# Summing edge attributes two chunks at a time in a graph network kernel: 64 or 128 stationary columns per product

## The chip, the cores and the metric

The kernel runs on one core of a Trainium2 chip. The metric is the device time of one execution in microseconds (us), as the median of a few runs. Five engines work side by side: TensorE (PE in the profile, with its weight loads in a row of their own, PEld), VectorE (DVE), ScalarE (ACT), GpSimd (POOL) and SyncE (SP), which here only issues transfers.

## The reference, cut to what matters

A graph with 6,250 nodes and 206,250 edges (self loops among them, sorted by destination) goes through two residual blocks. The first is two graph convolutions, the second an MLP whose input for each node is its own 128 features, the sum of the 64 attributes of all edges that end in it, and a constant vector.

```python
agg = jax.ops.segment_sum(edge_attr, col, num_segments=x.shape[0])   # (206250, 64) -> (6250, 64)
h = jnp.concatenate([x, agg, u[batch]], axis=1)
h = leaky_relu(h @ w1 + b1)
h = leaky_relu(h @ w2 + b2)
return h @ w3 + b3
```

The change is about `agg`, and about the one product of the MLP that reads it. All of this is in float32.

## The kernel before, in words

The program has stages that are separated by barriers.

**The first stage** does two things at once. One is the sum `agg`. The other is preparation: ScalarE counts where each node's edges begin (`count_rows`, `recount_rows`), GpSimd gathers rows of the edge list for it with indirect transfers (`rows`), VectorE and ScalarE normalise the nodes (`stats`, `mean_var`, `shift`, `h`), TensorE turns them (`turn_nodes`), and ScalarE and GpSimd split them into two halves in float16 (`scaled`, `g_hi`, `g_lo`).

For the sum the edges are cut into 162 runs of 1280 edges. A run lies on 128 partitions with 10 edges each, and "chunk" c of a run is the c-th edge of every partition, 128 edges with 64 attributes. The edges are sorted, so a run touches few nodes: VectorE compares each edge's destination, taken relative to the run's first, with 0..43 and gets a 0/1 matrix `hot` of 128 x 44 for each chunk (`make_hot`). TensorE multiplies the chunk's attributes (`arows`, the stationary operand, 64 columns) with the chunk's `hot` (the moving operand, 64 columns, of which 44 count) and adds the ten chunks of a run up in PSUM (`agg_p`). VectorE then adds the 44 columns into the resident sum `agg` at the run's first node (`add_unit`), which it reads from `base_i` into a register. The adds of two runs can touch the same nodes, so each waits for the one before it (`s_moved`).

Three runs are a unit, six units are a turn, and nine turns cover all edges: 54 units. The units are written out in the same order on each engine. SP loads the attributes of a unit (0.96 MB) into one of 6 buffers, VectorE makes `hot` two units ahead into one of 3 buffers, TensorE sums a unit in `sum_unit` into one of 3 banks. Before a unit TensorE waits for the load, for `hot` and for VectorE's adds of the unit three before. Part of the units stand in loops, and from the third turn on (the fourth for TensorE) they are written out singly, numbered m on VectorE and TensorE, with preparation work put between them: `stats` after m = 0 to 6, `mean_var` at 7, `shift` at 14, the edge codes at 15 and 16, transposes of nodes on TensorE from m = 15 on. The last turn runs in a loop of its own after all of this.

**The last stage**, the second layer with the MLP, goes over the nodes in 13 steps (one of 128 nodes, then 12 of 512). In each step TensorE does 98 products for the second convolution (`multiply`), and the short products of the MLP for the step before are put between them (`stages`). The one that reads `agg` is in `turn_to_nodes`. The weights come in `load_weights`, from SP's queue, and every engine waits for all of them (`s_w`).

Between these two lie the building of the adjacency matrix and the first convolution, which the change does not touch.

Of the kernel before, what the change touches and what calls it, by code (L numbers as in the profile page):

```python
# [17 lines left out]
ALU = mybir.AluOpType  # L18
ACT = mybir.ActivationFunctionType
AX = mybir.AxisListType  # L20
F32 = mybir.dt.float32
# [4 lines left out]
P = 128  # L26
N, F = 6250, 128
E = 206250
HI = -(-N // P)
NP = HI * P  # L30
# [21 lines left out]
AC = 10  # L52
AE = P * AC
AT = -(-E // AE)
OVER = AT * AE - E
AH = AT // 2
AW = 44
AQ = 3
AU = 6
AS = 3  # L60
AK = 512 // AH
TURNS = AT // (AQ * AU)
TA, TB_, TC_, TC = 2, 3, 7, 7
# [2 lines left out]
GB = 5  # L66
SPLIT = [(k, min(GB, HI - k)) for k in range(0, HI, GB)]
EF = 64
HOT = AQ * AC * AW + EF - AW

EC = E // P
ET = E - P * EC
# [10 lines left out]
EPS = 1e-5  # L83
ROUNDS = -(-E // P) + 1
AROUNDS = -(-NP // AW)
assert OVER % AC == 0 and 0 < OVER < AE and TURNS * AQ * AU == AT and TC == TURNS - 2 and AU % AS == 0


def build(nc, x, src, dst, attr, W1, b1, W2, b2, u, w1, c1, w2, c2, w3, c3, out):
    with ExitStack() as top:  # L90
        def sb(name, shape, dt, ctx=top):
            return ctx.enter_context(nc.sbuf_tensor(name, shape, dt))

        def ps(name, shape, ctx):
            return ctx.enter_context(nc.psum_tensor(name, shape, F32))
# [25 lines left out]
        scale2 = sb("scale2", [P, 1], F32)  # L121
        inv2 = sb("inv2", [P, 1], F32)
        W1_sb = sb("W1_sb", [P, F], F32)
        agg = sb("agg", [EF, NP + AW], F32)
        b1_sb = sb("b1_sb", [P, 1], F32)

        class Chain:
# [92 lines left out]
        with ExitStack() as ph:  # L220
# [35 lines left out]
            arows = sb("arows", [P, AU, AQ, AC, EF], F32, ph)  # L256
            hot = sb("ahot", [P, AS, HOT], F32, ph)
            arel = hot[0:AH, :, :].rearrange("q s n -> q (s n)")[:, 0:2 * AE].rearrange("q (t e) -> q t e", t=2)
# [7 lines left out]
            agg_p = ps("agg_p", [P, AS, 512], ph)  # L266
# [44 lines left out]
            s_w = sem("s_w1", ph)  # L311
# [10 lines left out]
            s_moved = sem("s_moved", ph)  # L322
# [125 lines left out]
            def _(dve):  # L448
# [12 lines left out]
                def add_unit(r, i, k):  # L461

                    n = (r * TURNS + i) * AU + k
                    at = [dve.value_load(base_i[0:1, bass.ds((i * AU + k) * AQ + q, 1)], min_val=0, max_val=NP)
                          for q in range(AQ)]
                    dve.wait_ge(s_summed, n + (AU + 1))
                    for q in range(AQ):
                        dve.wait_ge(s_moved, n * AQ + (q + AS * AQ))
                        nc.vector.tensor_tensor(agg[:, bass.ds(at[q], AW)], agg[:, bass.ds(at[q], AW)],  # L469
                                                agg_p[0:EF, k % AS, q * EF:q * EF + AW], ALU.add).then_inc(s_moved, 1)  # L470

                def unit(i, k):

# [123 lines left out]
                with dve.Fori(0, rounds) as r:  # L597
                    start = first_turn(dve, r)
# [133 lines left out]
            def _(pe):  # L732
                pe.sem_inc(s_summed, AU)

                def sum_unit(r, i, k):
                    n = (r * TURNS + i) * AU + k
                    gate(pe, s_loaded[k], (r * TURNS + i + 1) * (32 if k == 0 else 16))
                    gate(pe, s_hot, n + 1)
                    gate(pe, s_moved, n * AQ + AQ)
                    for q in range(AQ):  # L740
                        for c in range(AC):
                            e = (q * AC + c) * AW
                            ins = nc.tensor.matmul(agg_p[0:EF, k % AS, q * EF:(q + 1) * EF], arows[:, k, q, c, :],  # L743
                                                   hot[:, k % AS, e:e + EF], start=(c == 0), stop=(c == AC - 1))
                    ins.then_inc(s_summed, 1)

                def sum_turns(a, b):
# [19 lines left out]
                for f, (t, c, n) in enumerate(AFILL):  # L767
# [3 lines left out]
                    for k in range(n):  # L771
                        ins = nc.tensor.transpose(tp[:, f % 2, k * AH:(k + 1) * AH],
                                                  arel[:, t, :].rearrange("q (p c) -> q c p", c=AC)[:, c + k, :],
                                                  ident[0:AH, 0:AH])
# [36 lines left out]
                with pe.Fori(0, rounds) as r:  # L811
                    start = first_turn(pe, r)
# [394 lines left out]
        def second_layer_and_mlp():  # L1207
# [3 lines left out]
            M1, M2 = w1.shape[1] // P, w2.shape[1] // P  # L1211
            assert M1 == M2
            KU = F + EF
# [5 lines left out]
            with ExitStack() as ph:  # L1219
# [20 lines left out]
                W_sb = sb("W2_sb", [P, F], F32, ph)  # L1240
                b_sb = sb("b2_sb", [P, 1], F32, ph)
                w1a = sb("w1a", [P, M1 * P], F32, ph)
                w1b = sb("w1b", [EF, M1 * P], F32, ph)
                w1u = sb("w1u", [EF, M1 * P], F32, ph)
                w2_sb = sb("w2_sb", [P, M1, M2 * P], F32, ph)
                w3_sb = sb("w3_sb", [P, M2, F], F32, ph)
# [11 lines left out]
                s_w = sem("s_w2", ph)  # L1258
# [48 lines left out]
                @block.sync  # L1307
                def _(sp):
                    def load_weights(sp):
                        sp.dma_start(W_sb[:, :], W2).then_inc(s_w, 16)  # L1310
                        sp.dma_start(w1a[:, :], w1[0:F, :]).then_inc(s_w, 16)
                        sp.dma_start(w1b[:, :], w1[F:KU, :]).then_inc(s_w, 16)
                        sp.dma_start(w1u[:, :], w1[KU:KU + EF, :]).then_inc(s_w, 16)
                        sp.dma_start(w2_sb[:, :, :], w2.rearrange("(m p) n -> p m n", p=P)).then_inc(s_w, 16)
                        sp.dma_start(w3_sb[:, :, :], w3.rearrange("(m p) n -> p m n", p=P)).then_inc(s_w, 16)
                        with nc.allow_non_contiguous_dma(reason="vectors, one element per partition"):
                            sp.dma_start(b_sb[:, :], b2.rearrange("(p a) -> p a", a=1)).then_inc(s_w, 16)  # L1317
                            sp.dma_start(c3_sb[:, :], c3.rearrange("(p a) -> p a", a=1)).then_inc(s_w, 16)
                            sp.dma_start(u_sb[:, :], u[0:1, :].rearrange("a n -> n a")).then_inc(s_w, 16)
                            sp.dma_start(c1_sb[:, :], c1.rearrange("(m p) -> p m", p=P)).then_inc(s_w, 16)  # L1320
                            sp.dma_start(c2_sb[:, :], c2.rearrange("(m p) -> p m", p=P)).then_inc(s_w, 16)

                    def program(sp, one_round):
                        def load(i, h, n):
                            c = i * 2 + h
                            w = n * P
                            cols = bass.ds(first_node(i, h), w)
                            if one_round and two_before(i):

                                gate(sp, dense_done, c + 1)  # L1330
                                sp.dma_start(adj_in[:, h, :, 0:w], adj_d[:, :, cols]).then_inc(adj_ready[h], 16)

                            if two_before(i):
                                gate(sp, y_added, c + 1)
                                gate(sp, stored[h], i * 16)
                            sp.dma_start(cur[:, h, 0:w], h1T_d[:, cols]).then_inc(small_ready[h], 16)
                            sp.dma_start(h0[:, h, 0:w], hT_d[:, cols]).then_inc(small_ready[h], 16)  # L1337
                            sp.dma_start(disb[:, h, 0:w],  # L1338
                                         dis_d[cols].rearrange("(a n) -> a n", a=1).to_broadcast([P, w])
                                         ).then_inc(small_ready[h], 16)  # L1340
                            if n == NT:
                                sp.dma_start(xt[:, h, :, :],
                                             x[bass.ds(first_node(i, h), CW), :].rearrange("(c p) f -> p c f", p=P)
                                             ).then_inc(small_ready[h], 16)
                            else:
                                sp.wait_ge(s_pad, 1)
                                sp.dma_start(xt[0:TAIL, h, 0, :], x[(HI - 1) * P:N, :]).then_inc(small_ready[h], 16)
                            if not one_round:
                                sp.dma_start(tot[:, h, 0:w], total_d[:, cols]).then_inc(small_ready[h], 16)

                        load(0, 0, 1)
                        load(0, 1, NT)
                        load_weights(sp)
                        with sp.Fori(1, NC // 2) as i:
                            for h in range(2):
                                load(i, h, NT)
                        load(NC // 2, 0, NT)

                    by_rounds(sp, program)
# [19 lines left out]
                def _(dve):  # L1379
# [1 line left out]
                    dve.sem_inc(mixed, 2)  # L1381
                    nc.vector.memset(xt[:, 0, 0, :], 0.0).then_inc(s_pad, 1)

                    dve.wait_ge(s_w, 16 * 11)
                    dve.wait_ge(s_uc, 1)
                    nc.vector.tensor_tensor(c1_sb[:, :], c1_sb[:, :], lin_p[:, 0:M1], ALU.add).then_inc(s_c1, 1)

# [70 lines left out]

                @block.scalar
                def _(act):  # L1460
                    act.wait_ge(s_w, 16 * 11)
                    act.wait_ge(s_c1, 1)

                    def program(act, one_round):
# [45 lines left out]
                def _(pe):  # L1510
                    pe.sem_inc(dense_done, 2)

                    def u_product():
                        pe.wait_ge(s_w, 16 * 11)
                        for q in range(M1):
                            ins = nc.tensor.matmul(lin_p[:, q:q + 1], w1u[:, q * P:(q + 1) * P], u_sb[:, :],
                                                   start=True, stop=True)
                        ins.then_inc(s_uc, 1)
                        pe.wait_ge(s_c1, 1)
# [143 lines left out]
```

## Time and profile before

| | us |
|---|---|
| median of 3 runs | 1205.93 (1205.38 to 1206.0) |
| span of the profiled execution | 1226.5 |
| TensorE matmul busy in it | 1087.3 (89%) |
| TensorE weight loads busy in it | 713.1 (58%) |
| VectorE busy in it | 721.1 (59%) |
| ScalarE busy in it | 603.0 (49%) |
| first stage, to VectorE's last instruction | about 285 |
| last stage, from its first transfer | about 799 to 1226 |

The profiled execution has a span of 1226.5 us, from its first to its last instruction. The page gives no time of its own beside that span, and the span is 20.6 us more than the median of the timed runs. Engine shares are averages over stages with different limits, so each stage has to be read by itself.

### The profile page before, as it was taken

The page shows a single profiled execution, that of the slowest core. Times are in us where ns is not written, and L with a number is a line of the kernel's source. Part 1 is how long each engine was busy: PE and PEld are TensorE (multiplying, and loading weights), DVE is VectorE, ACT ScalarE, POOL GpSimd, SP SyncE. Part 2 cuts the span into 40 slices and gives each one's busy share as a digit, 9 for nine tenths or more (in the row PEclk, how much of TensorE's full clock was granted, in tenths as well). Part 3 has the DMA queues.
Part 4 walks back from the last instruction along what each step waited for, and adds up shares of the span by engine and source line. Part 5 has one row for each costly group of instructions (what it writes and reads, how often), then busy time and mean ns, then how long its engine had stood idle before and what let it go on. Part 6 is the DMA issues. An engine that isn't in the chain of part 4 may idle for free. (4 is left out here: it accounts for less than half of the span.)

```text
span 1226.5 us, 29959 instructions
## 1 busy us (share of the span) xinstructions
PE 1087.3 (89%) x9678; PEld 713.1 (58%) x9679; DVE 721.1 (59%) x1190; ACT 603.0 (49%) x1353; POOL 273.8 (22%) x195
## 2 busy tenths in 40 slices
PE   4777999985799999999999995479999999999995
PEld 3766998984666666666666652244444444444442
DVE  4433876644999999999999935612333332223323
ACT  3989125613788888888888842401122211221222
POOL 3745000435594222222232003100000000000000
PEclk9977999986799999999999997779999999999997
DMA  6975789840356555555555569967677777777710
GB/s 221 312 246 170 251 273 331 282 137 17 116 185 204 189 193 192 193 192 193 192 193 192 192 202 282 337 196 237 216 233 237 230 233 246 240 237 246 245 42 17
DMA packets 227114, 255.86 MB, mean 209 GB/s; under 512 B 14106, under 2 KB 192399, under 8 KB 226920
## 3 DMA queue, kind: packets, MB, share of 16 engines
q1 hardware_dynamic: 112244, 147.77, 37.8%
q10 hardware_dynamic: 109828, 96.49, 24.4%
q0 software_dynamic: 4976, 10.71, 2.8%
q8 instruction: 42, 0.69, 0.2%
q14 instruction: 24, 0.20, 0.0%
HBM read 164.95 MB, written 90.00 MB: 208 GB/s over the span
## 5 line engine op out<-in xcount | busy, mean ns | idle before, releaser
L977 ACT CAST adj_all<-win_p 128x392 f32 x784 | 340.2, 499 | 55.2 <-issue 33.2
L1027 PEld LDWEIGHTS win_p<-adj_all,st 128*128 128x128 f16 x3136 | 214.4, 101 | 145.6 <-ACT adj_all L977 30.4
L1027 PE MATMUL win_p<-adj_all,st 128*128 128x98 f16 x3136 | 255.7, 212 | 23.9 <-ACT adj_all L977 17.3
L926 DVE TENSOR_TENSOR st<-iota_lo,code 128x2048 f16 x196 | 243.4, 1242 | 15.9 <-ACT code L966 8.1
L1589 PE MATMUL dense_p_b<-adj_all,g_hi 128*128 128x512 f16 (+1 forms) x637 | 231.3, 371 | 18.4 <-issue 18.0
L743 PE MATMUL agg_p<-ahot,arows 128*64 128x64 f32 x3240 | 216.7, 232 | 32.4 <-issue 24.3
L1042 PE MATMUL dense_p<-adj_all,g_hi 128*128 128x448 f16 x686 | 240.6, 351 | 1.4 <-DVE total L937 0.7
L1042 PE MATMUL dense_p<-adj_all,g_lo 128*128 128x448 f16 x686 | 241.2, 352 | 0.0
L743 PEld LDWEIGHTS agg_p<-ahot,arows 128*64 128x64 f32 x3240 | 209.5, 147 | 39.9 <-issue 38.9
L1589 PE MATMUL dense_p_b<-adj_all,g_lo 128*128 128x512 f16 (+1 forms) x637 | 231.1, 371 | 0.0
L926 DVE TENSOR_TENSOR adj_all<-iota_mv,code 128x1568 f16 x196 | 192.1, 980 | 0.0
L1589 PEld LDWEIGHTS dense_p_b<-adj_all,g_hi 128*128 128x128 f16 x637 | 63.4, 100 | 97.7 <-issue 38.1
L1589 PEld LDWEIGHTS dense_p_b<-adj_all,g_lo 128*128 128x128 f16 x637 | 63.5, 100 | 74.8 <-issue 15.4
L1489 ACT ACTIVATE z<-zz_p,c_sb 128x512 f32<-128x512 f32 (+1 forms) x52 | 34.2, 662 | 145.3 <-PE zz_p L1551 83.8
L469 DVE TENSOR_TENSOR agg<-agg,agg_p 64x44 f32 x162 | 31.3, 193 | 119.7 <-PE agg_p L743 64.4
L1365 POOL DMA_DIRECT2D out_dram<-xt x12 | 9.1, 760 | 373.3 <-DVE xt L1446 373.3
L1439 DVE SCALAR_TENSOR_TENSOR a<-z 128x512 f32<-128x512 f32 (+1 forms) x52 | 34.3, 661 | 93.9 <-ACT z L1489 93.9
L174 POOL CAST start_i<-start 112x2 int32 (+1 forms) x16 | 55.2, 3449 | 147.3 <-PE code_p L1015 147.2
L455 DVE TENSOR_TENSOR ahot<-iota_w,relT 128x1320 f32<-128x1320 f32 x54 | 84.6, 1573 | 2.8 <-issue 2.2
L1042 PEld LDWEIGHTS dense_p<-adj_all,g_hi 128*128 128x128 f16 x686 | 67.2, 98 | 7.8 <-issue 1.9
L627 ACT ACTIVATE cmp<-heads_b,tgt 128x1375 f16<-128x1375 int16 x49 | 69.8, 1427 | 0.0
L1042 PEld LDWEIGHTS dense_p<-adj_all,g_lo 128*128 128x128 f16 x686 | 65.9, 96 | 4.4
(189 smaller groups left out, 883.4 us busy)
## 6 DMA issues: line engine op xcount, KB each, us to landing
adj_d<-adj_all ACTq DMA_DIRECT2D x14, 5488.0 KB, 19.5
adj_all<-adj_d SPq DMA_DIRECT2D x11, 6272.0 KB, 23.5
arows<-in_edge_attr_dram SPq DMA_DIRECT2D x45, 960.0 KB
adj_all<-adj_d ACTq DMA_DIRECT2D x1, 6272.0 KB, 35.3
disb<-dis_d SPq DMA_DIRECT2D x24, 256.0 KB, 5.3
arows<-in_edge_attr_dram SPq DMA_DIRECT2D x9, 640.0 KB
h<-in_x_dram ACTq DMA_DIRECT2D x4, 768.0 KB
hT_d<-hT ACTq DMA_DIRECT2D x12, 256.0 KB, 5.7
```

The costliest lines, as they stand in the source:

```text
L174: nc.gpsimd.tensor_copy(start_i[:, h, :], start[:, bass.ds(i * 4 + 2 * h, 2)]).then_inc(indices, 1)
L455: nc.vector.tensor_tensor(hot[:, k % AS, 0:AQ * AC * AW].rearrange("p (e n) -> p e n", n=AW), iota_w[:, :].unsqueeze(1).to_broadcast([P, A ...
L469: nc.vector.tensor_tensor(agg[:, bass.ds(at[q], AW)], agg[:, bass.ds(at[q], AW)], agg_p[0:EF, k % AS, q * EF:q * EF + AW], ALU.add).then_i ...
L627: nc.scalar.activation(cmp[:, k % CR, :], heads_b[:, :], ACT.Sign, bias=tgt[:, k:k + 1], scale=-1.0, accum_out=sign[:, k:k + 1]).then_inc( ...
L743: ins = nc.tensor.matmul(agg_p[0:EF, k % AS, q * EF:(q + 1) * EF], arows[:, k, q, c, :], hot[:, k % AS, e:e + EF], start=(c == 0), stop=(c ...
L926: ins = nc.vector.tensor_tensor(hot[:, bass.ds((b * BG + j) % 2, 1), u, :, :] .rearrange("p a w (n t) -> p (a w) n t", t=2), iota[:, :].re ...
L977: nc.scalar.copy(adj[:, bass.ds(b % 2, 1), :, bass.ds(j * GN + k * WN, WN)] .rearrange("p b h d -> p (b h) d"), win_p[:, k % 4, 0:WP * MV] ...
L1027: ins = nc.tensor.matmul(win_p[:, k % 4, 0:WP * MV] .rearrange("p (h c t) -> p h c t", c=WP, t=PN)[:, :, c, :], st[:, odd, k // UW, pair, ...
L1042: ins = nc.tensor.matmul(dense_p[:, half, 0:BN], g[:, c, :], adj[:, half, c, :], start=(c == 0 and g is g_hi), stop=(c == HI - 1 and g is ...
L1439: nc.vector.scalar_tensor_tensor(out=a[:, q, 0:w], in0=z[:, q, 0:w], scalar=SLOPE, in1=z[:, q, 0:w], op0=ALU.mult, op1=ALU.max).then_inc(a ...
L1489: nc.scalar.activation(z[:, q, 0:w], zz_p[:, q, 0:w], ACT.Identity, bias=bias[:, q:q + 1]).then_inc(z_ready, 1)
L1589: ins = nc.tensor.matmul(dense_p[:, h, 0:n * P], g[:, k, :], adj_in[:, h, k, 0:n * P], start=(k == 0 and g is g_hi), stop=(k == HI - 1 and ...
```

## The change

Two neighbouring chunks of a run become the stationary operand of one product: 128 columns, the attributes of chunk c and then those of chunk c + 1. The moving operand is the two `hot` blocks side by side, 88 columns. The result is 128 x 88. In its rows 0 to 63 and columns 0 to 43 stands the sum for chunk c, in rows 64 to 127 and columns 44 to 87 that for chunk c + 1; the other two quarters are products of one chunk's attributes with the other's `hot`, and are not read. `agg` gets a second partition half: VectorE adds the one block into the lower half and the other into the upper half, two instructions where there was one, with a wait only before the first of them. In the last stage `w1b`, the weights of the aggregated attributes, is loaded twice, once for each half, so that the product over 128 rows joins the halves.

```diff
-HOT = AQ * AC * AW + EF - AW
+HOT = AQ * AC * AW
+AD = 2 * AW
...
-        agg = sb("agg", [EF, NP + AW], F32)
+        agg = sb("agg", [P, NP + AW], F32)
...
                     for q in range(AQ):
                         dve.wait_ge(s_moved, n * AQ + (q + AS * AQ))
-                        nc.vector.tensor_tensor(agg[:, bass.ds(at[q], AW)], agg[:, bass.ds(at[q], AW)],
-                                                agg_p[0:EF, k % AS, q * EF:q * EF + AW], ALU.add).then_inc(s_moved, 1)
+                        for d in range(2):
+                            side = slice(d * EF, d * EF + EF)
+                            ins = nc.vector.tensor_tensor(
+                                agg[side, bass.ds(at[q], AW)], agg[side, bass.ds(at[q], AW)],
+                                agg_p[side, k % AS, q * AD + d * AW:q * AD + (d + 1) * AW], ALU.add)
+                        ins.then_inc(s_moved, 1)
...
                     for q in range(AQ):
-                        for c in range(AC):
+                        for c in range(0, AC, 2):
                             e = (q * AC + c) * AW
-                            ins = nc.tensor.matmul(agg_p[0:EF, k % AS, q * EF:(q + 1) * EF], arows[:, k, q, c, :],
-                                                   hot[:, k % AS, e:e + EF], start=(c == 0), stop=(c == AC - 1))
+                            ins = nc.tensor.matmul(agg_p[:, k % AS, q * AD:(q + 1) * AD],
+                                                   arows[:, k, q, c:c + 2, :].rearrange("p c f -> p (c f)"),
+                                                   hot[:, k % AS, e:e + AD], start=(c == 0), stop=(c == AC - 2))
                     ins.then_inc(s_summed, 1)
...
-                w1b = sb("w1b", [EF, M1 * P], F32, ph)
+                w1b = sb("w1b", [P, M1 * P], F32, ph)
...
-                        sp.dma_start(w1b[:, :], w1[F:KU, :]).then_inc(s_w, 16)
+                        for d in range(2):
+                            sp.dma_start(w1b[d * EF:(d + 1) * EF, :], w1[F:KU, :]).then_inc(s_w, 16)
...
-                    dve.wait_ge(s_w, 16 * 11)
+                    dve.wait_ge(s_w, 16 * 12)
```

The wait for the weights goes from 11 to 12 loads on ScalarE and TensorE too.

On VectorE, the adds of the first unit inside the loop over the first turns stand so before the change: a read of `base_i` into a register, then one add for each of the three runs. The row printed as ISA right before an add waits for the add before (`s_moved`).

```order
L464 TENSOR_LOAD base_i
L464 ISA x2
L466 REGISTER_ALU
L468 REGISTER_ALU
L469 ISA
L469 TENSOR_TENSOR agg<-agg,agg_p 64x44
L468 REGISTER_ALU
L469 ISA
L469 TENSOR_TENSOR agg<-agg,agg_p 64x44
L468 REGISTER_ALU
L469 ISA
L469 TENSOR_TENSOR agg<-agg,agg_p 64x44
```

After the change the same place reads as follows, up to the second run's adds. The ISA before the first add of a run waits as before, the one before the second add doesn't.

```order
L465 TENSOR_LOAD base_i
L465 ISA x2
L467 REGISTER_ALU
L469 REGISTER_ALU
L472 ISA
L472 TENSOR_TENSOR agg<-agg,agg_p 64x44
L472 ISA
L472 TENSOR_TENSOR agg<-agg,agg_p 64x44
L469 REGISTER_ALU
L472 ISA
L472 TENSOR_TENSOR agg<-agg,agg_p 64x44
L472 ISA
```

Each run now has two adds in place of one, six in a unit in place of three; the rest of the unit is as it was.

On TensorE the units written out singly, where node transposes stand between them, read so before the change.

```order
L743 MATMUL agg_p<-ahot,arows 64x64 x300
L758 MATMUL tp<-ident,h 128x128 x4
L743 MATMUL agg_p<-ahot,arows 64x64 x30
L758 MATMUL tp<-ident,h 128x128 x4
L743 MATMUL agg_p<-ahot,arows 64x64 x30
```

And so after it.

```order
L748 MATMUL agg_p<-ahot,arows 128x88 x150
L764 MATMUL tp<-ident,h 128x128 x4
L748 MATMUL agg_p<-ahot,arows 128x88 x15
L764 MATMUL tp<-ident,h 128x128 x4
L748 MATMUL agg_p<-ahot,arows 128x88 x15
```

A unit is 15 products where it was 30, and nothing moved past anything else. In the trace each float32 product is two records, two weight loads and two matmuls, so a unit shows 60 records before.

## Rows read from the trace of the kernel before

**Rows 1.** The page: span, and the costliest groups of the sum.

```profile
span 1226.5 us, 29959 instructions
...
L743 PE MATMUL agg_p<-ahot,arows 128*64 128x64 f32 x3240 | 216.7, 232 | 32.4 <-issue 24.3
...
L469 DVE TENSOR_TENSOR agg<-agg,agg_p 64x44 f32 x162 | 31.3, 193 | 119.7 <-PE agg_p L743 64.4
```

**Rows 2.** Busy time by stretch of the first stage, instructions in brackets.

```profile
26.00:51.00 25.00, 24.90 (x400) 24.69 (x401) 14.26 (x26) 24.93 (x39) 13.97 (x10) 1.00 0.94 316
68.00:125.00 57.00, 43.79 (x489) 40.39 (x487) 19.21 (x46) 46.55 (x122) 29.17 (x28) 0.77 0.67 220
125.00:184.00 59.00, 58.19 (x951) 57.41 (x952) 47.10 (x162) 11.77 (x34) 0.00 (x0) 0.98 0.83 270
184.00:230.00 46.00, 44.27 (x669) 41.90 (x667) 26.13 (x65) 23.36 (x58) 3.14 (x5) 1.00 0.96 320
230.00:254.00 24.00, 23.73 (x407) 23.59 (x405) 14.04 (x28) 18.31 (x49) 15.62 (x10) 1.00 0.85 278
```

**Rows 3.** Timeline of TensorE's sum, at full and at half clock (start, length).

```profile
213.81 2.73 PE L743 MATMUL agg_p<-ahot,arows 128*64 128x64 f32 x44
...
258.38 3.86 PE L743 MATMUL agg_p<-ahot,arows 128*64 128x64 f32 x34 [4.65 <-DVE ahot L455]
```

**Rows 4.** Timeline of weight loads with 128 float32 columns.

```profile
184.68 0.30 PEld L787 LDWEIGHTS small_p<-cnt,below 128*128 128x128 f32 x2
184.90 0.30 PEld L788 LDWEIGHTS small_p<-cnt,corner 128*128 128x128 f32 x2
...
812.97 0.52 PEld L1516 LDWEIGHTS lin_p<-u_sb,w1u 64*128 64x128 f32 x4 [2.60 <-DMA c_sb<-in_L_gnn_b_dram]
```

**Rows 5.** Timeline of VectorE, two units with nothing between them.

```profile
149.24 0.85 DVE L469 TENSOR_TENSOR agg<-agg,agg_p 64x44 f32 x3 [0.43 <-issue]
150.01 1.52 DVE L455 TENSOR_TENSOR ahot<-iota_w,relT 128x1320 f32<-128x1320 f32 x1
151.98 0.85 DVE L469 TENSOR_TENSOR agg<-agg,agg_p 64x44 f32 x3 [0.46 <-issue]
```

**Rows 6.** Timeline of TensorE and GpSimd in a stall.

```profile
64.60 0.35 PE L743 MATMUL agg_p<-ahot,arows 128*64 128x64 f32 x1 [1.16 <-issue]
65.31 0.26 PE L743 MATMUL agg_p<-ahot,arows 128*64 128x64 f32 x1 [0.36 <-issue]
...
64.18 0.94 POOL L420 DMA_INDIRECT rows<-in_dst_dram,row_i  x1 [0.30 <-issue]
```

**Rows 7.** The sum's instructions in four stretches between stalls: the first, and the total.

```profile
67.40:76.00 8.60, 8.38 (x95) 8.23 (x95) 0.67 0.89 264
...
sum 36.00, PE 35.74 PEld 35.14; mean PE 8.93 PEld 8.78
```

**Rows 8.** Timeline of the ends of the first stage on GpSimd and VectorE.

```profile
283.03 0.87 POOL L190 TENSOR_SCALAR ql<-ql 112x256 f32<-112x256 f32 x1 [0.20 <-POOL ql L184]
...
285.25 0.16 DVE L615 RECIPROCAL scale<-inv 128x1 f32<-128x1 f32 x1
```

**Rows 9.** The chain that ended last, in the last stage (start, length, work).

```profile
804.29 0.56 SPq L1312
...
845.33 0.52 PE tpa L1534 x4
845.85 1.91 PE zz_p L1539 x4
847.76 7.45 PE dense_p_b L1589 x34
855.20 0.44 PE tpb L1545 x4
855.64 1.29 PE dense_p_b L1589 x6
856.93 1.72 PE zz_p L1551 x4
```

More of the change, by code:

```diff
@@ L85 @@
 AROUNDS = -(-NP // AW)
-assert OVER % AC == 0 and 0 < OVER < AE and TURNS * AQ * AU == AT and TC == TURNS - 2 and AU % AS == 0
+assert OVER % AC == 0 and 0 < OVER < AE and TURNS * AQ * AU == AT and TC == TURNS - 2 and AU % AS == 0 and AC % 2 == 0
 def build(nc, x, src, dst, attr, W1, b1, W2, b2, u, w1, c1, w2, c2, w3, c3, out):
@@ L1460, in _ @@
                 def _(act):
-                    act.wait_ge(s_w, 16 * 11)
+                    act.wait_ge(s_w, 16 * 12)
                     act.wait_ge(s_c1, 1)
@@ L1513, in u_product @@
                     def u_product():
-                        pe.wait_ge(s_w, 16 * 11)
+                        pe.wait_ge(s_w, 16 * 12)
                         for q in range(M1):
```

## Prediction

> **What bounds the kernel now.** I read the page first, then the busy time by stretch, then the timelines of the first stage, and last the chain that ended last. The page gives the size of what is touched: 3240 records of the sum's matmuls keep TensorE busy for 216.7 us of a span of 1226.5, and 162 adds cost VectorE 31.3 us [rows 1]. At two records a product and 30 products a unit that is 54 units.
>
> The table by stretch shows that the first stage has several limits [rows 2]. From 26 to 51 us TensorE works without a gap at full clock (24.90 of 25 us). From 68 to 125 us the granted clock is 0.77, and only 489 records are done in 57 us. From 125 to 184 TensorE is busy again for 58.19 of 59 us, and VectorE for 47.10. From 184 to 254 TensorE is busy for 68 of 70 us and VectorE has room (40 us).
>
> Between 51 and 125 us TensorE stalls several times: it starts one matmul per 0.7 us (64.60, then 65.31), and waits for nothing that the trace shows ("issue"), while GpSimd issues its gathers of `rows` [rows 6]. After such a stall the clock is low. A record at full clock comes every (2.73 - 0.22)/43 = 58.4 ns, with 0.22 us for the last one's own length (the mean of all, those at half clock too, is 0.23 [rows 1]); at half clock every (3.86 - 0.33)/33 = 107 ns [rows 3], with 0.33 for the last one (single ones are 0.26 to 0.35 [rows 6]). The latter is 64 columns, twice, at 1.2 GHz. In the four stretches between stalls there are 433 records in 35.7 us [rows 7]; with a share f at half clock, 433 x (58.4 + 48.6 f) = 35,740 gives f = 0.50, half of them at half clock.
>
> The first stage ends on VectorE at 285.4 us, but GpSimd ends at 283.9, only 1.5 us before it [rows 8].
>
> In the last stage the chain is TensorE nearly throughout. The product with `w1b` takes 1.91 us for four records there, the product with `w1a`, of the same width, 1.72 [rows 9].
>
> **TensorE's part of the sum.** Products halve, but each weight load has 128 columns in place of 64, and the moving side 88 in place of 64. A float32 product is two records. The moving side of a record would take 58.4 x 88/64 = 80 ns at full clock. The weight side has a row: four loads of 128 float32 columns start between 184.68 and 185.01, two in each of two rows of 0.30 us, 0.22 apart. That is 110 ns per load, though only 49 columns move in between (two loads 0.11 apart in 0.30 us leave 0.19 for the length of one) [rows 4]. So 80 ns is the lower bound of a record and 110 the value that the nearest row gives; I take 110. A unit then goes from 60 x 58.4 = 3.50 us to 30 x 110 = 3.30, a gain of 0.20 us and no more (2.4 us would be 80 ns; the row speaks against it). At half clock the row at 812.97, right after a long idle time, shows the same pitch, (0.52 - 0.19)/3 = 110 ns [rows 4], so there the moving side decides, 107 x 88/64 = 147 ns: a unit goes from 6.42 us to 4.41.
>
> The Trainium skill, page "TensorE: Matmul & The Clock Gate", section "LDWEIGHTS (loading the stationary operand)", says that a load takes its columns divided by 1.2 in ns, whatever the contraction rows are. By this rule 128 columns are 107 ns, the trace's 110 agrees, and since the change loads as many columns in all as before (640 per pass of a run) it speaks against any large gain; a unit would be 3.2 us by it.
>
> By stretch: 26 to 51 us, 400 records, 6.7 units x 0.20 = -1.3. Between stalls, where f = 0.5: 216 records at half clock save 107 - 147/2 = 33.5 ns each, -7.2 us, and the 217 at full clock 3.4 ns, -0.7. How much of these 7.9 arrives is open, since the stalls and VectorE stand between; both ends are 0 and -7.9, and if the stalls count instructions rather than time, more (below). I take half, -4, because the median is 20.6 us below the profiled span, and stalls without a visible cause are the likeliest thing to be shorter in unprofiled runs. From 184 to 254: 1076 records less 49 transposes are 17 units, -3.4.
>
> **VectorE's part.** Three more adds per unit. The page's mean of one is 193 ns [rows 1]. Three linked adds take 0.85 us, so a wait makes the pitch (0.85 - 0.19)/2 = 0.33 us. The new second adds don't wait. Without a wait, `hot` starts 0.77 us after the first of the adds, 0.08 before the last ends [rows 5], so an unlinked instruction costs 0.19 - 0.08 = 0.11 us. I take 0.11, 0.34 per unit; the upper bound is 0.28 (the linked pitch without its wait), 0.85 per unit. VectorE's own pace goes from 151.98 - 149.24 = 2.74 us per unit [rows 5] to 3.08, or to 3.59 at the upper bound.
>
> Where does that show? From 125 to 184 us: 951 records are 15.9 units; VectorE is busy 47.10 us [rows 2] and stands 0.43 us per unit before the adds while it reads registers (the idle times in [rows 5]), 6.8 in all, sum 53.9. Adding 15.9 x 0.34 = 5.4 makes 59.3 of 59 us. So this stretch, with its normalisation work, becomes VectorE's, and TensorE's 3.2 us are not gained: I put it at +1. Behind the adds stands the next `hot`, and TensorE waits for it. From 184 on, VectorE has 40 us of work plus 17 x 0.77 = 13 in 70; it stays hidden.
>
> **Transposes between units.** Thirteen times TensorE goes from the 64-column sum to 128-column transposes and back. I take this with the effect in the last stage, below: about 0.15 us each, -2.
>
> **Last turn.** Six units, -1.2, and its first 34 records are at half clock (3.86 us), -1.1; VectorE's last adds +0.3. But GpSimd would then end last: only -1.5 of this counts [rows 8]. Work that GpSimd does before hangs on ScalarE's halves and the transposes, so it moves with the earlier gains.
>
> First stage: -1.3 - 4 + 1 - 3.4 - 2 - 1.5 = -11.2. Since these terms share one path with VectorE and ScalarE and will not all add up, I take -9.
>
> **Last stage.** After 64 contraction rows become 128, `w1b` looks like `w1a`. The chain gives three differences per step [rows 9]: 1.91 against 1.72 us; the four transposes before it 0.52 against 0.44 for the same four at 855.20; and the 34 products behind it 7.45 against 34 x 1.29/6 = 7.31. Sum 0.41 us. Over 12 steps this is -4.9 if all of it comes from the change of shape, 0 if none; I take 0.35 x 12 = -4.2. Against it stands one more transfer issue on the chain, `w1b`'s 0.56 us plus 0.04 [rows 9]: +0.6. Together -3.6.
>
> The Trainium skill, page "TensorEngine Tiling (Array Packing)", section "Tiling Modes", says that changing the tiling mode drains TensorE. By it the differences above are drains, and both here and at the transposes of the first stage they should go. No row isolates a drain.
>
> **Sum.** -9 - 3.6 = -12.6, against the profiled span 1226.5 -> 1214, and against the median 1205.9 -> 1193.5.
>
> **Rivals.**
> 1. As above, 1193.5, own range 1189 to 1199: 0.40.
> 2. The stalls between 51 and 125 us count instructions. If TensorE gets so many instructions and no more while GpSimd gathers, half as many per unit means twice the work before and in each stall. All 7.9 us then arrive, and in the stalls 3 or so units more are done than before, less what VectorE's pace of 3.08 allows: another 4 to 10. Time 1182 to 1189: 0.17. For it: "issue" as the only cause. Against it: VectorE stalls too.
> 3. VectorE takes most of it. With the upper bound of 0.28 us per second add its unit is 3.59 us, above the 3.50 of before. From 26 to 51 us that is +0.6 in place of -1.3, and from 125 to 184 it needs 53.9 + 15.9 x 0.85 = 67.4 us, +8.4. From 184 on it needs 40 + 7.3 + 14.5 = 62 of 70 us, so that TensorE's gains there stay. With the other terms (-4, -3.4, -2, -1.5, -3.6) this is -5.5, or 1199 to 1203. For it: each add carries an address from a register. Against it: so does `hot` in [rows 5]. 0.20.
> 4. The change doesn't do what it says: with some overhead the loads' 110 ns fill a unit as before (116 ns would), and the last stage's differences have another cause, so that the issue's +0.6 is left: -1 to +0.8, 1205 to 1206.7. 0.11.
> 5. Slower: the loads of 128 columns don't run beside 88 moving float32 columns as they do beside 49. Each record then takes more than either side alone; at the full sum it would be 190 ns. At 130 ns a unit is 3.9 us, +0.4 over 45.6 units outside the stalls (+18), less 4 there and 3.6 in the last stage: 1216. It decides from 120 ns on, where 45.6 x 0.1 = 4.6 us pay back the last stage's gain. For it: the sum has no such pair yet. Against it: four transposes of 128 float32 columns, each with its load, take 0.44 us, 110 ns each [rows 9]. 0.12.
>
> **From this to the numbers.** About 0.2% (2.4 us) is what a measurement of this kernel can tell from no change. Faster: 1, 2 and nearly all of 3, 0.75; same: 4 and the end of 3, 0.12; slower: 5 and a little of 4, 0.13. The range for 8 in 10 goes from 1184 to 1207: it leaves out the lower half of rival 2 (0.08) and rival 5 (0.12).
>
> **What would show it.** Weight loads of the sum 110 ns apart in full-clock stretches, a unit 3.3 us, at half clock 147 ns. Adds in pairs 0.11 us apart. From 125 us on VectorE without idle time until the edge codes are done. In the last stage four records of `w1b` in 1.72 us and each step some 0.35 us shorter. It is wrong if a unit stays at 3.5 us, if TensorE waits for `hot` from 184 us on, or if the stalls take the same instructions as before and the stage starts its late part at the same unit.

## The result

The changed kernel takes 1275.89 us, median of 4 runs (1273.63 to 1277.1), against 1205.66 before (1202.72 to 1206.0). The ratio is 1.0589, with a 95% interval of 1.0573 to 1.0605: 70 us slower. I had forecast 1193.5, with a range of 1184 to 1207.

The page of the changed kernel names the place. These are its span and the costliest groups of the sum, as in [rows 1].

```profile
span 1271.9 us, 27044 instructions
...
L748 PE MATMUL agg_p<-ahot,arows 128*128 128x88 f32 x1620 | 290.9, 370 | 11.3 <-DVE ahot L456 11.0
L748 PEld LDWEIGHTS agg_p<-ahot,arows 128*128 128x128 f32 x1620 | 289.6, 284 | 12.1 <-issue 12.0
...
L472 DVE TENSOR_TENSOR agg<-agg,agg_p 64x44 f32 x324 | 64.3, 198 | 134.9 <-PE agg_p L748 102.9
```

The records of the sum halved from 3240 to 1620, as the change says, but they keep TensorE busy for 290.9 us in place of 216.7. The mean weight load is 284 ns long, where the loads of this width in [rows 4] are 190. VectorE's adds doubled, and VectorE waits for TensorE 102.9 us, where it was 64.4.

By stretch (length, then busy time of PE, PEld, DVE, ACT and POOL, granted clock, DMA share, GB/s), beside [rows 2]:

```profile
26.00:51.00 25.00, 25.00 (x119) 25.00 (x119) 10.38 (x23) 24.93 (x39) 12.34 (x12) 1.00 0.83 270
...
125.00:184.00 59.00, 59.00 (x279) 59.00 (x278) 34.83 (x143) 4.46 (x16) 0.00 (x0) 1.00 0.49 161
...
230.00:254.00 24.00, 23.05 (x202) 22.24 (x201) 18.67 (x55) 15.68 (x37) 1.94 (x4) 1.00 0.92 302
300.00:320.00 20.00, 20.00 (x96) 20.00 (x95) 8.17 (x21) 0.00 (x0) 5.98 (x7) 0.50 0.05 13
```

Divide length by records. From 26 to 51 us a record takes 25/119 = 210 ns, from 125 to 184 us 211, from 300 to 320 us 208; only from 230 to 254 us, with transposes among them, is it 24/202 = 119. The last row's granted clock is 0.50, which is the 1.2 GHz level. Work of the same shape at the same pace, with weight loads that fill the whole stretch, means that the stretches before 204 us ran at half clock too. The 1.00 printed there doesn't fit this pace. The column seems to have no record of the clock before its first change, and this kernel's first change is late. The timeline of TensorE shows where it comes:

```profile
179.72 25.38 PE L748 MATMUL agg_p<-ahot,arows 128*128 128x88 f32 x118
204.90 1.06 PE L764 MATMUL tp<-ident,h 128*128 128x128 f32 x4
205.75 4.25 PE L748 MATMUL agg_p<-ahot,arows 128*128 128x88 f32 x30
209.84 0.60 PE L764 MATMUL tp<-ident,h 128*128 128x128 f32 x4
210.28 3.48 PE L748 MATMUL agg_p<-ahot,arows 128*128 128x88 f32 x30
213.59 0.60 PE L764 MATMUL tp<-ident,h 128*128 128x128 f32 x4
214.03 3.48 PE L748 MATMUL agg_p<-ahot,arows 128*128 128x88 f32 x30
218.87 0.66 PE L764 MATMUL tp<-ident,h 128*128 128x128 f32 x4 [1.36 <-ACT h L696]
220.27 0.42 PE L793 MATMUL small_p<-cnt,below 128*128 128x49 f32 x2 [0.74 <-DVE cnt L555]
...
220.86 6.39 PE L748 MATMUL agg_p<-ahot,arows 128*128 128x88 f32 x30
...
227.88 3.48 PE L748 MATMUL agg_p<-ahot,arows 128*128 128x88 f32 x30
```

Up to 204.90 us the 88-column products run at 210 ns, for 179 us on end and without idle time. Then come the first transposes, whose moving side is 128 columns. Within the next unit the pace changes, and from 210.28 on a unit of 30 records takes 213.59 - 210.28 = 3.31 us, which is 110 ns each, the value I had forecast for full clock. The clock is lost once more, after idle times of 1.36 and 0.74 us with four transposes between them: the unit at 220.86 takes 6.18 us until the next transposes at 227.04, and from 227.88 on a unit is fast again. From 295.4 to 334 us, in the last turn, where no transposes come, all 180 records run at a granted clock of 0.50.

The last stage did what was forecast. From the chain that ended last, to be laid beside [rows 9]:

```profile
893.88 0.52 PE tpa L1541 x4
894.40 1.72 PE zz_p L1546 x4
896.12 7.34 PE dense_p_b L1596 x34
```

The product that reads `agg` is down from 1.91 to 1.72 us, the 34 products behind it from 7.45 to 7.34; the transposes ahead of it stay at 0.52. That is 0.30 per step.

### The profile page after: what moved, and what is told of

Its sections match the earlier page's. It is cut to its first block and busy times, and to the rows that moved or that the text cites. A ratio compares the mean times of both kernels' runs of the same rounds, so it can differ in the third digit from the quotient of the medians.

```text
span 1271.9 us, 27044 instructions
## 1 busy us (share of the span) xinstructions
PE 1158.7 (91%) x8058; PEld 795.9 (63%) x8059; DVE 756.6 (59%) x1352; ACT 603.6 (47%) x1353; POOL 268.5 (21%) x195
## 5 line engine op out<-in xcount | busy, mean ns | idle before, releaser
L748 PE MATMUL agg_p<-ahot,arows 128*128 128x88 f32 x1620 | 290.9, 370 | 11.3 <-DVE ahot L456 11.0
L748 PEld LDWEIGHTS agg_p<-ahot,arows 128*128 128x128 f32 x1620 | 289.6, 284 | 12.1 <-issue 12.0
L472 DVE TENSOR_TENSOR agg<-agg,agg_p 64x44 f32 x324 | 64.3, 198 | 134.9 <-PE agg_p L748 102.9
```

Source lines behind the costliest of these rows:

```text
L472: ins = nc.vector.tensor_tensor(agg[side, bass.ds(at[q], AW)], agg[side, bass.ds(at[q], AW)], agg_p[side, k % AS, q * AD + d * AW:q * AD + ...
L748: ins = nc.tensor.matmul(agg_p[:, k % AS, q * AD:(q + 1) * AD], arows[:, k, q, c:c + 2, :].rearrange("p c f -> p (c f)"), hot[:, k % AS, e ...
```

## The experiments

All comparisons are with the kernel before, timed beside each run: 1203.24 us beside the first four below, 1204.0 us beside the others.

### 128 moving columns

The products keep their 128 stationary columns, and the moving side gets as long. The results of the 40 surplus columns are not read.

```diff
-HOT = AQ * AC * AW
-AD = 2 * AW
+HOT = AQ * AC * AW + 2 * EF - 2 * AW
+AD = 2 * EF
```

> The changed kernel, but 128 moving columns in place of 88 (the surplus columns are neighbours of the wanted ones or zeros, and their results are not read). Nothing else differs: as many products, as many stationary columns. In the changed kernel a record of the sum comes every 210 ns from 26 to 225 us and again from 300 to 334, and every 111 ns in between, with a granted clock that rises only when transposes come. Theory A (clock): a load of 128 float32 columns takes 110 ns at full clock and twice that at half clock, so at half clock the load side sets the pace, the moving side runs for 147 of 210 ns, and with that the clock is not granted back. With 128 moving columns the moving side is as long as the load (128 twice at 1.2 GHz is 213 ns), the clock should rise as it does before the change, and a unit should take 3.3 us: first stage ended near 270 us, median 1190 to 1210. Theory B (the loads from the attribute buffers are slow for another reason, whatever the moving side does): pitch stays 210 ns, median 1270 to 1280. Theory C (work on TensorE per unit is simply more): slower than the changed kernel, over 1280.

Measured: 1212.37 us, ratio 1.0071 (1.0047 to 1.0095). Giving TensorE 45% more columns to move takes 63 us off the changed kernel. The groups of the sum over the whole run (duration in ns, min/median/max, then first and last start) and its first stretches:

```profile
L748 PEld LDWEIGHTS agg_p<-ahot,arows x1620: 186/192/338, 25.6 to 269.7; 128*128 128x128 f32 x180
L748 PE MATMUL agg_p<-ahot,arows x1620: 274/275/551, 25.6 to 269.8; 128*128 128x128 f32 x180
...
26.00:51.00 25.00, 25.00 (x207) 25.00 (x207) 15.73 (x37) 24.93 (x39) 13.99 (x11) 1.00 0.92 316
```

The median load is 192 ns long, not 333 as in the changed kernel, and 207 records fit where 119 did. Theory A holds against B and C: neither the loads' width nor their source buffer alone makes them slow.

What remains of the loss is on VectorE, as its timeline shows.

```profile
107.32 1.52 DVE L456 TENSOR_TENSOR ahot<-iota_w,relT 128x1320 f32<-128x1320 f32 x1
108.87 1.51 DVE L472 TENSOR_TENSOR agg<-agg,agg_p 64x44 f32 x6
110.41 1.45 DVE L525 BATCH_NORM_STATS2 stats<-h 128x6 f32<-128x128 f32 x7
111.78 1.51 DVE L456 TENSOR_TENSOR ahot<-iota_w,relT 128x1320 f32<-128x1320 f32 x1
```

One unit follows the other without idle time, 111.78 - 107.32 = 4.46 us each, while TensorE needs 3.3 and waits. The six adds take 1.51 us against 0.85 for three. The same units in the kernel before come every 3.56 us (profiled again, below).

### 44 moving columns in the kernel before

The opposite edit: 64 stationary columns and single adds as before, and the moving side cut from 64 to the 44 columns that count.

```diff
-agg_p[0:EF, k % AS, q * EF:(q + 1) * EF], arows[:, k, q, c, :], hot[:, k % AS, e:e + EF]
+agg_p[0:EF, k % AS, q * EF:q * EF + AW], arows[:, k, q, c, :], hot[:, k % AS, e:e + AW]
```

> The kernel before, but 44 moving columns in place of 64 (the 20 surplus columns are left out, they were never read). 64 stationary columns, 30 products and single adds as before. Theory A: at half clock the load of 64 float32 columns takes 107 ns and the moving side only 73, so the clock is not granted here either, and a unit takes 60 x 107 = 6.4 us: the first stage gets as long as in the changed kernel, median 1260 to 1285, slower although TensorE is given less to do. Theory B or C (the 128 stationary columns are at fault): same as before or up to 5 us faster, 1195 to 1207.

Measured: 1336.27 us, ratio 1.1095 (1.1059 to 1.113), even longer than I had expected. The same two views:

```profile
L743 PEld LDWEIGHTS agg_p<-ahot,arows x3240: 179/227/232, 25.9 to 393.2; 128*64 128x64 f32 x191
...
25.94 34.34 PE L743 MATMUL agg_p<-ahot,arows 128*64 128x44 f32 x320 [3.14 <-DVE ahot L455]
...
236.64 1.12 PE L758 MATMUL tp<-ident,h 128*128 128x128 f32 x4
237.68 6.63 PE L743 MATMUL agg_p<-ahot,arows 128*64 128x44 f32 x60
244.24 1.12 PE L758 MATMUL tp<-ident,h 128*128 128x128 f32 x4
```

A record comes every 34.34/320 = 107 ns, and the sum ends at 393 us. Here no load is wider than before the change, there are no second adds, and the last stage is untouched. In this kernel the transposes don't bring the clock back either. They stand at 13 places and it rises at none; with transposes on both sides a unit of 60 records takes 244.24 - 237.68 = 6.56 us, where the changed kernel had got to 3.31.

### A dense start

Twelve products of 512 moving columns ahead of the first unit of the changed kernel.

```diff
+                gate(pe, s_loaded[0], 32)
+                for _ in range(12):
+                    nc.tensor.matmul(norm_p[:, :], ident[:, :],
+                                     arows[:, 0, 0, 0:8, :].rearrange("p c f -> p (c f)"), start=True, stop=True)
                 sum_turns(0, TB_)
```

> The changed kernel, with 12 products of 512 moving columns put ahead of the first unit (their result is not read), and nothing after that. It asks whether the clock, once at full, stays there under the 88-column products. Theory A in its form that a stream of such products can hold the clock but not raise it: from about 35 us on a record every 111 ns until the first idle time of TensorE of some us, then again half clock; between 25 and 70 us faster than the changed kernel, median 1215 to 1262. Theory A in its other form, that the clock falls under them anyway: half clock again within some us, median 1275 to 1285. Theory B: no change but the products' own time, 1280.

Measured: 1252.93 us, ratio 1.0424 (1.0379 to 1.0469): 23 us less than the changed kernel although it does more. TensorE's timeline and one stretch:

```profile
23.97 11.06 PE L755 MATMUL norm_p<-arows,ident 128*128 128x512 f32 x23
34.87 25.36 PE L748 MATMUL agg_p<-ahot,arows 128*128 128x88 f32 x226
...
92.90 7.52 PE L748 MATMUL agg_p<-ahot,arows 128*128 128x88 f32 x34 [7.15 <-DVE ahot L456]
...
125.00:184.00 59.00, 59.00 (x279) 59.00 (x278) 31.52 (x130) 12.91 (x50) 6.24 (x7) 0.50 0.48 160
```

After the dense start a record takes 25.36/226 = 112 ns, and the pace holds under the 88-column products through waits of up to 0.81 us, until TensorE sits idle for 7.15 us, waiting for `hot`. After that 34 records take 7.52 us, and from 125 to 184 us there are 279 of them at 211 ns, in the same number as in the changed kernel, this time with a granted clock of 0.50 printed. So this stream kept the clock once it had it, and once it was lost it did not get it back in 89 us without a gap. This run also has the same load at either level in one kernel: 112 ns a record at full clock, 211 at half.

### Second adds alone

The kernel before, with VectorE's part of the change only. The second add reads an unused half of PSUM into an upper half of `agg` that nothing reads.

```diff
-nc.vector.tensor_tensor(agg[:, ...], agg[:, ...], agg_p[0:EF, k % AS, q * EF:q * EF + AW], ALU.add).then_inc(s_moved, 1)
+for d in range(2):
+    side = slice(d * EF, d * EF + EF)
+    ins = nc.vector.tensor_tensor(agg[side, ...], agg[side, ...], agg_p[side, k % AS, q * EF:q * EF + AW], ALU.add)
+ins.then_inc(s_moved, 1)
```

> The kernel before with the second add of each run put in, from the unused upper half of PSUM into an upper half of the sum that is not read afterwards; products and last stage as before. It prices VectorE's part alone. In the changed kernel six adds take 1.51 us against 0.85 for three, 0.22 per second add. With TensorE at full clock this makes VectorE's own pace 3.4 us per unit and should show in the stretches where VectorE also normalises: +4 to +12 us. If VectorE hides it: within 2 us of before.

Measured: 1217.13 us, ratio 1.0103 (1.0071 to 1.0136), +14 us by the medians and +12 by the ratio, at or a little over the upper end of what I had expected. VectorE doesn't hide them. Its timeline between two units:

```profile
133.73 1.51 DVE L471 TENSOR_TENSOR agg<-agg,agg_p 64x44 f32 x6 [0.26 <-issue]
135.27 1.53 DVE L455 TENSOR_TENSOR ahot<-iota_w,relT 128x1320 f32<-128x1320 f32 x1
137.06 1.50 DVE L471 TENSOR_TENSOR agg<-agg,agg_p 64x44 f32 x6 [0.25 <-issue]
```

VectorE's own pace, with nothing else between, is 137.06 - 133.73 = 3.33 us per unit. In [rows 5] it was 2.74. That is 0.59 more for three adds. TensorE needs 3.50, so anything that VectorE has to do beside a unit now delays TensorE.

### The kernel before, profiled again

Unchanged, for its profile.

> The kernel before, unchanged, with a profile of its own. Its first profiled execution spans 1226.5 us, 20 us more than the timed runs, and shows TensorE starting one matmul per 0.7 us from 51.7 to 67.4 us. Both kernels with a profile near their timed runs (128 moving columns; second adds alone) show no such stall. If that stall belonged to the one profiled execution, this one spans 1199 to 1206 us and has at most short idle times between 51 and 68 us. If it belongs to the kernel: a span near 1225 again.

Measured: 1205.79 us, with a span of 1204.1. Busy time in three stretches:

```profile
51.00:68.00 17.00, 17.00 (x295) 17.00 (x294) 10.37 (x21) 16.69 (x35) 13.96 (x11) 1.00 1.05 365
...
91.40:95.00 3.60, 3.58 (x34) 3.60 (x35) 2.95 (x11) 3.60 (x7) 0.00 (x0) 0.50 0.10 40
95.00:121.00 26.00, 26.00 (x446) 26.00 (x445) 24.09 (x121) 25.93 (x59) 18.04 (x13) 0.99 0.82 275
```

From 51 to 68 us TensorE is busy throughout, with 295 records where the first profile had stalls. Its one long idle time in the sum comes later, and has a cause that the trace names. These are VectorE and TensorE there, and then two adds of VectorE in the units behind it:

```profile
89.50 1.53 DVE L455 TENSOR_TENSOR ahot<-iota_w,relT 128x1320 f32<-128x1320 f32 x1 [18.05 <-DMA h<-in_x_dram]
...
91.42 29.92 PE L743 MATMUL agg_p<-ahot,arows 128*64 128x64 f32 x480 [13.94 <-DVE ahot L455]
...
95.35 0.84 DVE L469 TENSOR_TENSOR agg<-agg,agg_p 64x44 f32 x3
...
98.91 0.84 DVE L469 TENSOR_TENSOR agg<-agg,agg_p 64x44 f32 x3
```

VectorE stands for 18.05 us until the nodes (`h`) have been loaded, and TensorE, which has used up the `hot` matrices, stands for 13.94. In the changed kernel neither waits here. After its idle time TensorE's stream is at half clock (0.50, with 34 records in 3.6 us) and is back at 0.99 from 95 us on, with nothing but its own 64-column products. That is the place to lay beside the dense start, where the 88-column products stayed at 0.50. The seven units with `stats` that follow take 98.91 - 95.35 = 3.56 us each on VectorE, already a little more than TensorE's 3.50.

VectorE's last instruction of the stage ends at 260.5 us in this one, not at 285.4:

```profile
260.35 0.16 DVE L615 RECIPROCAL scale<-inv 128x1 f32<-128x1 f32 x1
```

In the changed kernel it starts at 336.66. The stalls of [rows 6] and [rows 7], on which I had built a term and a rival, belonged to one profiled execution. VectorE's part of the first stage grew by 76 us and not by the 51 that the first profile gives. TensorE's first product of the next stage moves by less, from 266.14 to 338.75 us, 72.6 later.

### The last stage alone

The kernel before with the 128-row product over an upper half of `agg` that stays zero, and the second load of the weights.

```diff
-w1b = sb("w1b", [EF, M1 * P], F32, ph)
+w1b = sb("w1b", [P, M1 * P], F32, ph)
...
-sp.dma_start(w1b[:, :], w1[F:KU, :]).then_inc(s_w, 16)
+for d in range(2):
+    sp.dma_start(w1b[d * EF:(d + 1) * EF, :], w1[F:KU, :]).then_inc(s_w, 16)
```

> The kernel before, with the change's last stage alone: the second copy of the attribute weights and a product over 128 rows, of which the upper 64 multiply an upper half of the sum that stays zero. The first stage sums and adds as before. In the changed kernel the four records of this product take 1.72 us in place of 1.91, and the 34 products behind them 7.34 in place of 7.45. If this comes from the shape: 12 or 13 steps x 0.30 = -3.6 to -3.9 us, and +0.6 for the issue: -3 us, median ratio 0.9975. If TensorE's order of the first stage has a part in it: no change beyond +0.6.

Measured: 1201.12 us, ratio 0.9974 (0.9961 to 0.9988), as expected. It is the one version here that computes the whole sum and beats both kernels. Its chain has the changed kernel's times:

```profile
821.48 1.72 PE zz_p L1540 x4
823.20 7.34 PE dense_p_b L1590 x34
```

### 128 moving columns, without the second adds

```diff
-                        for d in range(2):
+                        for d in range(1):
```

> The changed kernel with 128 moving columns, and without the second add of each run, so that the chunks of odd number are left out of the sum. It leaves TensorE's part alone, at the clock of before, and the last stage's. If VectorE's adds are all that is left of the loss at 128 moving columns (+8.6 us against before, where the adds alone cost +13): 1196 to 1201, that is -3 for the last stage and 0 to -6 for TensorE's 0.14 to 0.2 us per unit. If the 128-column products cost something of their own: above 1204.

The chunks of odd number are left out of the sum here, so this prices work and is no usable kernel. Measured: 1197.33 us, ratio 0.9947 (0.9928 to 0.9967), within what I had expected. The weight loads of its sum, busy time from 127 to 145 us, TensorE after the wait for `h`, and VectorE's last instruction of the stage:

```profile
L748 PEld LDWEIGHTS agg_p<-ahot,arows x1620: 186/192/334, 25.5 to 253.7; 128*128 128x128 f32 x180
...
127.00:145.00 18.00, 18.00 (x162) 18.00 (x162) 11.95 (x29) 8.07 (x35) 6.77 (x6) 0.99 0.81 265
...
92.26 29.23 PE L748 MATMUL agg_p<-ahot,arows 128*128 128x128 f32 x240 [16.68 <-DVE ahot L456]
...
256.37 0.16 DVE L620 RECIPROCAL scale<-inv 128x1 f32<-128x1 f32 x1
```

A record takes 18/162 = 111 ns, as at 88 columns and full clock, and VectorE has time to spare. VectorE's last instruction starts at 256.37 us, against 260.35 in the unchanged kernel (and 258.85 in the kernel with the new last stage alone, whose first stage is the unchanged one, so part of the 4 us is spread between executions). TensorE's faster sum ahead of the wait for `h` bought nothing: the idle time grew from 13.94 to 16.68 us, and the sum went on at 92.26 instead of 91.42.

## Why the prediction was wrong

The medians account for the loss in steps. From the changed kernel (1275.9) to 128 moving columns (1212.4) the clock gives back 63.5 us. From there to single adds (1197.3) VectorE gives back 15.0. What is left lies 6.7 us below the kernel before (1204.0 beside that run), of which the last stage, measured alone, is 2.9. The remaining 3.8 us are what is left for TensorE's products in the first stage. The intervals of the two runs make this anything from about 1 to 7 us, and that is all that "half the products" was worth.

**The step that failed: the granted clock was taken as given.** The prediction asks what a record costs at the level that the profile of before shows in each stretch, and puts at nothing, without a reason, what the change does to the level itself. No term and no rival has it. The runs show that this is the loss: the 848 records before 204.8 us and the 180 of the last turn came every 210 ns instead of 110, by estimate 103 us of TensorE's time, and as many products with 128 moving columns give 63.5 us back. (One part of the difference is that the slow sum has no idle time at the load of `h`, where the kernel before has 13.94 us.)

**Under it, the half-clock price of a weight load was wrong too.** I wrote "At half clock the row at 812.97, right after a long idle time, shows the same pitch, 110 ns, so there the moving side decides, 147 ns". I had taken a long idle time for half clock without reading the granted clock of that row. The busy time of this stretch, in the kernel before, shows it:

```profile
812.90:813.60 0.70, 0.60 (x4) 0.52 (x4) 0.00 (x0) 0.00 (x0) 0.00 (x0) 1.00 0.00 0
```

It is 1.00, so the row was a second sight of full clock. At half clock a load of 128 float32 columns takes 210 ns. So the unit at half clock is 30 x 210 = 6.3 us, not 4.41, against 6.42 before, and the -7.2 us between the stalls, of which half went into the sum, and the -1.1 in the last turn had nothing under them.

**Which streams got the clock.** In the kernel before, at half clock, the moving side of a record (64 columns twice, 107 ns) is as long as its load, and the stream raised the clock by itself. With 88 columns behind a load of 128 the moving side takes 147 of 210 ns, and the clock stayed at half for the first 179 us of the sum, and for the last turn. The two opposite edits show that neither width alone decides: 128 moving columns beside 128 stationary ones have nearly the clock of before, and 44 beside 64 lose it. What exactly the chip counts I can't say from these runs. None of my rivals had this; rival 5 forecast a slower record too, but through loads that don't run beside the moving side, and at full clock the measured 110 ns refute it.

**TensorE's part at full clock** was right: 110 ns per record, 3.31 us per unit. What it was worth was not: the -1.3 us from 26 to 51 and the -4 between 51 and 125 lie ahead of, or around, the wait for `h`, which the first profile, with its stalls, did not show and which takes back what TensorE gains before it.

The Trainium skill, page "TensorE: Matmul & The Clock Gate", section "LDWEIGHTS (loading the stationary operand)", gives columns divided by 1.2 in ns and no clock beside it. At full clock the trace agrees (110 ns for 128 float32 columns, 107 by the rule); at half clock it doesn't (210 ns), and the measurement decides.

**VectorE's part** was right in kind and mis-sized. A second add costs (1.51 - 0.85)/3 = 0.22 us, twice the 0.11 that I took from the nearest row and within the bounds (0.11 to 0.28). With TensorE at full clock the adds cost 12 to 15 us, where I had +1 as a forecast and +8.4 in rival 3. The stretch was also not quite the one I had named. The units with `stats` go from 3.56 to 4.46 us, 0.90 more each and 6.3 for the seven. In the run with the second adds alone TensorE reaches the first transposes at 155.73 us instead of 147.06 (8.7 later), and the last turn at 249.66 instead of 235.45 (14.2 later). So more than a third arises behind the first transposes, where I had written that VectorE stays hidden.

**The stalls.** The half term of -4 us and rival 2 rested on what one execution showed. They are neither confirmed nor refuted as a mechanism; none of the later profiles has them, and the timed runs of the kernel before are as short as the profile without them.

**The transposes between units** gave more of TensorE's time than I had put down. In the kernel before, at full clock:

```profile
212.24 0.66 PE L758 MATMUL tp<-ident,h 128*128 128x128 f32 x4
212.83 3.71 PE L743 MATMUL agg_p<-ahot,arows 128*64 128x64 f32 x60
216.47 0.66 PE L758 MATMUL tp<-ident,h 128*128 128x128 f32 x4
```

Four transposes take 0.59 us here until the next unit starts, and the unit 3.64 where an unbroken stream needs 3.50. In the changed kernel they take 0.44 us (213.59 to 214.03) and the unit 3.31, with nothing lost at either side. That is 0.29 us each time where I had 0.15, an estimate of 3.8 us for thirteen. No run isolates what of it arrives in the time.

**The last stage** was forecast at -3.6 and gave -2.9 alone (interval -4.7 to -1.4). The differences of 0.19 and 0.11 us went away with the shape; the 0.08 at the transposes ahead did not. The Trainium skill, page "TensorEngine Tiling (Array Packing)", section "Tiling Modes", says that a change of the tiling mode drains TensorE. The first two differences agree with that and the third doesn't; no run here shows a drain by itself.

## What to carry to other kernels

Before making a product's stationary side wider than its moving side, look at what a record costs at half clock as well as at full, and whether the stream will still get the clock back after each idle time. Columns that are moved and thrown away can pay: here 40 surplus columns per product saved 63 us, and cutting 20 cost 133. A gain on one engine ahead of a wait for a load only makes the wait longer. And profile a kernel twice where its span is 20 us above its timed runs, before building terms on a stall.

## What was unexpected of the hardware

- The clock. A stream that kept TensorE busy without a gap from 26 to 205 us did not get the full clock: 88 moving columns, twice, behind loads of 128. It came within the unit behind the first four float32 transposes. Under 44 moving columns behind loads of 64, it came behind none of the 13 groups of transposes.
- The same stream held the clock once it had it (226 records at 112 ns after a dense start), and after one idle time of 7.15 us it was at half clock for the next 89 us. The kernel before, after 13.94 us of idle time at the same wait, was back at 0.99 from 95 us on. Shorter idle times lost the clock as well: 1.36 and 0.74 us around four transposes in the changed kernel.
- A load of 128 float32 columns follows the clock: 110 ns at full, 210 at half.
- The clock column shows 1.00 up to the first change that was recorded. In the changed kernel and in the one with 44 moving columns that does not fit the pace for 179 us and more, and only the length of the weight loads (333 in place of 190 ns, 227 in place of 138) gives it away.
